# Another order for the start of a two-layer kernel: x first, weight splits inside the first stage A, no clearing of the block diagonal

## The reference

```python
# block 1: linear attention
Q, K, V = x @ Wq.T + bq, x @ Wk.T + bk, x @ Wv.T + bv
Q, K = l2_norm(Q, rows), l2_norm(K, rows)     # over the 1024 rows
tailor = 1 / (256 + Q . (sum(K) + eps))
y = x + gamma * (value_sum + Q @ (K.T @ V)) * tailor
# block 2: all 8 experts, weights = softmax of the gate, cut below 0.1, made to sum to 1
y = sum_e weights[:, e] * (x @ expert_w[e] + expert_b[e])
# block 3: 16 heads of 16 columns; scores between the heads of one row (16 x 16)
y = softmax(q @ k.T / 8) @ v, then @ Wproj.T + bproj
# block 4: router picks the 768 of 1024 rows with the highest x . w_router;
#          these rows become gelu(x @ w_block), the others stay
```

## Time and profile before

| | us |
|---|---|
| median of 3 runs | 1647.24 (1645.47 to 1650.93) |
| profiled execution | 1648.01 |
| its span, first to last instruction | 1646.3 |
| PE busy / PE weight loads | 1253.3 / 793.0 |
| DVE, ACT, POOL busy | 956.6, 671.1, 612.8 |

### The profile page before, as it was taken

One profiled execution on the slowest core, in us unless ns is written; L12 is line 12 of the kernel. 1 busy time (PEld: TensorE's weight loads), 2 busy tenths in 40 slices (PEclk: granted clock), 3 DMA queues, 4 the chain that ended last, 5 costly groups with the idle time before them and its releaser, 6 DMA issues. The chain is left out here.

```text
span 1646.3 us, 33286 instructions
## 1 busy us (share of the span) xinstructions
PE 1253.3 (76%) x12232; PEld 793.0 (48%) x12232; DVE 956.6 (58%) x2185; ACT 671.1 (41%) x1164; POOL 612.8 (37%) x890
## 2 busy tenths in 40 slices
PE   0769987988699868988699877988699886675352
PEld 0445545645375435655375445655375444442341
DVE  2143566567464856567464865567464865574545
ACT  3022345236623446236623455236623445144523
POOL 3214346135443356135343256135343355134312
PEclk9869997899779897899869997899879997698566
DMA  4000062201802063201802073201802063207220
GB/s 133 13 13 8 20 126 30 66 7 71 118 3 65 14 137 47 65 8 71 118 3 65 14 138 45 65 8 71 118 3 52 1 135 45 53 1 138 42 53 26
DMA packets 92918, 90.78 MB, mean 55 GB/s; under 512 B 7031, under 2 KB 81721, under 8 KB 92474
## 3 DMA queue, kind: packets, MB, share of 16 engines
q1 hardware_dynamic: 90170, 79.93, 24.9%
q0 software_dynamic: 2560, 8.39, 1.5%
HBM read 46.35 MB, written 41.94 MB: 54 GB/s over the span
## 5 line engine op out<-in xcount | busy, mean ns | idle before, releaser
L1410 PE MATMUL bank<-we,at 128*128 128x512 f16 x1536 | 396.4, 422 | 100.0 <-issue 52.8
L1410 PEld LDWEIGHTS bank<-we,at 128*128 128x128 f16 x1536 | 161.5, 107 | 317.6 <-issue 129.6
L513 POOL TENSOR_TENSOR part<-part 128x512 f32<-128x512 f32 x64 | 81.2, 1268 | 355.5 <-ACTq L787 355.5
L651 ACT ACTIVATE part<-bank,wexp 128x256 f32<-128x256 f32 x256 | 104.9, 471 | 208.1 <-PE bank L1410 161.5
L1130 DVE SCALAR_TENSOR_TENSOR x<-bank,wexp,x 128x256 f32<-128x256 f32 x256 | 122.9, 480 | 62.1 <-PE bank L1410 52.1
L763 ACT ACTIVATE x<-x,nm,rs 128x256 f32<-128x256 f32 x192 | 104.4, 593 | 129.8 <-POOL nm L501 129.3
L1410 PE MATMUL bank<-bt,wqkv 128*128 128x512 f16 x576 | 138.4, 382 | 18.8 <-DVE stage L975 16.8
L975 DVE TENSOR_TENSOR stage<-bank,stage 128x512 f16<-128x512 f32 x128 | 86.6, 687 | 100.5 <-ACT stage L651 100.4
L651 ACT ACTIVATE blockdiag<-shared,const 128x2048 f16<-128x2048 f16 x64 | 122.7, 1990 | 35.6 <-POOL shared L545 34.7
L494 POOL TENSOR_SCALAR nm<-mv 128x2 f32<-128x2 f32 x128 | 29.7, 232 | 260.5 <-DVE mv L1007 256.2
L651 ACT ACTIVATE stage<-bank 128x512 f16<-128x512 f32 x128 | 75.5, 597 | 123.9 <-PE bank L1410 83.2
(11 more groups left out here) (176 smaller groups left out, 2236.1 us busy)
## 6 DMA issues: line engine op xcount, KB each, us to landing
scratch_qkv<-stage SPq DMA_DIRECT2D x48, 512.0 KB, 3.4
ct<-scratch_qkv SPq DMA_DIRECT2D x128, 128.0 KB, 5.7
x_in<-in_x_dram SPq DMA_DIRECT2D x32, 256.0 KB, 2.7
keys<-scratch_qkv SPq DMA_DIRECT2D x64, 128.0 KB, 10.8
scratch_o<-stage SPq DMA_DIRECT2D x64, 128.0 KB, 3.1
bt<-scratch_o SPq DMA_DIRECT2D x16, 512.0 KB, 3.7
out_dram<-x POOLq DMA_DIRECT2D x32, 256.0 KB, 2.6
blockdiag<-in_expert_w_dram SPq DMA_DIRECT2D x1, 2048.0 KB
```

The source lines that it names most:

```text
L513: pool.tensor_tensor(part[:, 0:2, :], part[:, 0:2, :], part[:, 2:4, :], ALU.add)\
L651: return act.activation(dst, src, ACT.Copy, scale=scale)
L1410: ins = pe.matmul(dst, lhs, rhs, start=(n == 0), stop=(n == len(terms) - 1))
```

## The change

SyncE's list now starts with the four loads of x. Six loads that stage A of batch 0 needs come next, on a semaphore of their own (`w_first`); the others follow in their old order on `w_loaded`. ScalarE and VectorE enter `turn` without waiting for the weights. In the turn that has only stage A, ScalarE makes `bvr` and the first four HI halves behind TX1 and the others behind IQ; VectorE makes the LO half of `we` before the copy of NORM, three more behind it, and the others behind `a_csum`. TensorE waits for `w_first` before srow, and for all halves before CB. GpSimd no longer clears `blockdiag`; its wait for `init_p` stands alone.

```diff
@@ sync @@
-            def load(dst, src):
-                sp.dma_start(dst, src).then_inc(w_loaded, 16)
-            load(const[:, :], consts)
...
+            def load(dst, src, loaded=w_loaded):
+                sp.dma_start(dst, src).then_inc(loaded, 16)
+            for p in range(TP):
+                load_x(0, p)
+            load(const[:, :], consts, w_first)
+            load(wqk[:, :, :], wqk_t.rearrange("(k p) n -> p k n", p=P), w_first)
+            load(brow[:, :], bqk[None, :], w_first)
+            load(gam[:, :], gamma[None, :].broadcast_to([P, 1]), w_first)
+            load(wvs[:, :, :], wv.rearrange("(k p) n -> p k n", p=P), w_first)
+            load(small[:, 1, :], bv, w_first)
+            load(small[:, 0, :], w_router)
...
-            for p in range(TP):
-                load_x(0, p)
             turn(1, None, None)
@@ gpsimd @@
-            pool.wait_ge(w_hi, N_SPLITS)
-            pool.wait_ge(w_lo, N_SPLITS)
-            pool.memset(wload, 0.0).then_inc(init_p, 1)
+            pool.wait_ge(init_p, 3)
@@ scalar @@
-            act.wait_ge(w_loaded, 16 * N_LOADS)
-            act.wait_ge(init_p, 3)
-            for w, src, scale in SPLITS:
-                copy(w[:, HI, :, :], src, scale).then_inc(w_hi, 1)
...
+            def bias_rows():
+                act.wait_ge(w_first, 16 * N_FIRST)
+                copy(bvr[:, :, :], small[:, 1, :, None].broadcast_to([P, KD, P])).then_inc(bvr_ready, 1)
+
+            def split_hi(ns):
+                act.wait_ge(w_loaded, 16 * N_LOADS)
+                act.wait_ge(init_p, 3)
+                for w, src, scale in SPLITS[ns]:
+                    copy(w[:, HI, :, :], src, scale).then_inc(w_hi, 1)
+                if ns.stop is None:
+                    copy(bproj16[0:1, :], rowin[0:1, 0:D])
+                    copy(gb16[0:1, :], rowin[0:1, D:D + E], WS)
+                    copy(rowtmp[32:33, 0:D], rowin[32:33, 0:D])
+                    copy(rowtmp[32:33, D:D + E], rowin[32:33, D:D + E], WS).then_inc(w_hi, 1)
@@ scalar, turn: behind to_at_hi(a, "TX1", 1, 1) @@
+                if b is None and c is None:
+                    bias_rows()
+                    split_hi(slice(0, 4))
@@ scalar, turn: behind a_iq(a) @@
+                if b is None and c is None:
+                    split_hi(slice(4, None))
@@ vector @@
+            def split_weights(ns):
+                dve.wait_ge(w_loaded, 16 * N_LOADS)
+                for n in ns:
+                    w, src, scale = SPLITS[n]
+                    dve.wait_ge(w_hi, n + 1)
+                    dve.scalar_tensor_tensor(out=w[:, LO, :, :], in0=src, scalar=scale, in1=w[:, HI, :, :],
+                                             op0=ALU.mult, op1=ALU.subtract).then_inc(w_lo, 1)
+                if ns.stop == N_SPLITS:
...
@@ vector, turn: ahead of a_norm(a), behind it, behind a_csum(a) @@
+                if b is None and c is None:
+                    split_weights(range(0, 1))
...
+                if b is None and c is None:
+                    split_weights(range(1, 4))
...
+                if b is None and c is None:
+                    split_weights(range(4, N_SPLITS))
@@ vector, ahead of turn(0, None, None) @@
+            dve.wait_ge(w_first, 16 * N_FIRST)
@@ tensor @@
             pe.wait_ge(init_p, 3)
-            pe.wait_ge(w_hi, N_SPLITS + 1)
-            pe.wait_ge(w_lo, N_SPLITS + 1)
@@ tensor, turn: ahead of a_srow(a), and ahead of a_cb(a) @@
+                if b is None and c is None:
+                    pe.wait_ge(w_first, 16 * N_FIRST)
...
+                if b is None and c is None:
+                    pe.wait_ge(bvr_ready, 1)
+                    pe.wait_ge(w_hi, N_SPLITS + 1)
+                    pe.wait_ge(w_lo, N_SPLITS + 1)
```

More of the change, by code:

```diff
@@ L150, in build_two_layer_postln @@
         a_bank, b_bank, m_bank = banks[0:2], banks[2:4], banks[4:8]
+        w_first = sem("w_first")
         w_loaded = sem("w_loaded")
+        bvr_ready = sem("bvr_ready")
         w_hi = sem("w_hi")
@@ L339, in build_two_layer_postln, with load_x @@
         N_SPLITS = len(SPLITS)
-        N_LOADS = 16 + T
+        N_FIRST, N_LOADS = 6, 10 + T
         @block.sync
         def _(sp):
-            def load(dst, src):
-                sp.dma_start(dst, src).then_inc(w_loaded, 16)
-            load(const[:, :], consts)
-            load(wqk[:, :, :], wqk_t.rearrange("(k p) n -> p k n", p=P))
-            load(wvs[:, :, :], wv.rearrange("(k p) n -> p k n", p=P))
+            def load(dst, src, loaded=w_loaded):
+                sp.dma_start(dst, src).then_inc(loaded, 16)
+            def load_x(a, p):
+                if later(a):
+                    sp.wait_ge(xs_lo, 4 * (a - 1) + p + 1)
+                    sp.sem_inc(waits_held, 1)
+                    sp.wait_ge(a_full, a_filled(a - 1, f"TX{p}"))
+                    sp.sem_inc(waits_held, 1)
+                sp.dma_start(x_in[:, 2 * p:2 * p + 2, :], x_d[a][:, 2 * p:2 * p + 2, :])\
+                    .then_inc(x_ready[p], 16)
+            for p in range(TP):
[6 more added lines that the diff above has]
+            load(small[:, 1, :], bv, w_first)
             load(small[:, 0, :], w_router)
-            load(small[:, 1, :], bv)
-            load(brow[:, :], bqk[None, :])
-            load(gam[:, :], gamma[None, :].broadcast_to([P, 1]))
             for r in (0, 32):
@@ L364, in _ @@
                 load(ebd_in[t * E:(t + 1) * E, t, :], expert_b)
[L366 to L373, removed]
             def b_f(b, k):
@@ L975, in split_lo @@
                 return dve.tensor_tensor(dst, src, hi, ALU.subtract)
[L978 to L987, removed]
+            def split_weights(ns):
[6 more added lines that the diff above has]
+                if ns.stop == N_SPLITS:
+                    dve.wait_ge(w_hi, N_SPLITS + 1)
+                    split_lo(bproj16[32:33, :], rowin[32:33, 0:D], rowtmp[32:33, 0:D])
+                    dve.scalar_tensor_tensor(out=gb16[32:33, :], in0=rowin[32:33, D:D + E], scalar=WS,
+                                             in1=rowtmp[32:33, D:D + E], op0=ALU.mult, op1=ALU.subtract)\
+                        .then_inc(w_lo, 1)
             done_a = StepCount(A_STEPS)
```

## The result

The changed kernel takes 1609.38 us (median of 4 runs, 1606.87 to 1616.0) beside 1647.36 us for the kernel before (4 runs, 1645.47 to 1650.93). The ratio is 0.9772 (95% interval 0.9745 to 0.9798), which is 38.0 us less. The forecast was 1609.5, in a range of 1604 to 1618. A second measurement, of 6 runs, gave 1609.56 (1607.39 to 1611.67; ratio 0.978, 0.9758 to 0.9803).

A forecast was written before the change was run, and what follows sets the result against it. The prediction took a serial prologue that idles TensorE until 50.44 us as the bound. Its terms, 40.0 - 0 - 2.3 = 37.7 us off the profiled 1648.01, gave 1610.3, set to 1609.5 for the median; range 1604 to 1618.

The forecast's parts named there:

- T0: Start of TensorE's first gram matmul, forecast to move from 50.47 to 10.4 us: 40.0 us gained (39.7 to 40.6).
- Operands and weights: Stage A's operands in by 11 us, all weights by 19 to 20, before they are asked for: no cost.
- The first part: Splits of we, wqkv, wproj and wblk before the first diagonal: cost 0, bounds 0 to +1.5 us.
- thin cover: VectorE free from the first splits only 0.15 us before G; any longer chain is paid in full.
- The second part: VectorE's splits of gw, wrt, ebd and bias rows behind scaled gt delay reading M: cost 2.3 us, bounds +1 to +3.5.
- rival 1: TensorE's clock falls elsewhere in the first stage A: 1619 us if earlier, 1606.5 if no fall; 15%.
- The large form: Clock falls before the stretch of T0, T1 and TROW, which takes up to twice its 9.4 us: 1619 us.
- The rest: Everything behind the first stage A moves 37.7 us earlier, with spans between batches as before.
- Rivals 2, 3 and 4: Gaps not covering splits, 1614 to 1619, 10%; waits leaving only the clearing's gain, 1633, 3%; slower loop, up to 1715, 2%.
- Late x: Part of rival 2, in front of the first gram: GpSimd's first x late by up to 2 us; whole rival 10%.
- rival 3: A wait makes first-batch work stand for the weights; only the clearing goes, 13.8 us, 1633 us; 3%.
- The slower loop: Loop bodies run at another phase with less clock granted; at 0.76 six passes lose 106 us, 1715 us; 2%.

The follow-up runs named there:

- e5: Changed kernel with VectorE's low half of the expert weights made twice, 4.42 us more in front of NORM's copy; 1614.12 us.
- e7: Kernel with late splits and x's low halves shared between GpSimd and VectorE, with low halves of wqkv, wproj and wblk also moved behind M; 1614.41 us.
- e3: Changed kernel with VectorE's second part of the low halves made behind M, later in the first stage A; 1609.13 us.
- e2: Changed kernel with the four loads of x issued behind all the others, as before the change; 1623.3 us.
- e1: Kernel before the change with only GpSimd's clearing of the block diagonal left out; 1633.46 us, ratio 0.9923.
- g4: Late-splits kernel with a row of its own for the bias rows, plus a 2.2 us GpSimd pause before x's low halves; 1614.41 us.
- g1: Late-splits kernel with x's low halves shared and an own bias row, plus a GpSimd pause behind those halves (2.9 us meant); 1616.19 us.

## Why the prediction was right

- *T0, 40.0 us forecast, 40.6 measured.* The term came out at its lower bound (5.2 + 4.74 = 9.9): the table load ran at 0.85 us and did not wait for x, so GpSimd's memsets bind. The value taken, 5.65 for the first high half, was 1.5 us too late (3.56 + 0.63 = 4.2). The sum by the Trainium skill's figure (ScalarE: Activation LUTs, What ACT_TABLE_LOAD costs), 1.4 us worse, did not come about. That says nothing against a drain of 1.38 us: the load was over at 2.13 us and the first activation followed 1.43 us later, when x had landed, so the trace has room for one and can't show it.
- *Operands and weights of no cost.* No wait for `w_first` or `w_loaded` shows: ScalarE went from `bvr` to `we` without a gap at 30.15.
- *The first part, 0 forecast with a thin cover; 0.6 measured, inside the bound of 0 to 1.5.* VectorE was predicted free at 41.1, and the diagonal follows the last split at 41.15. But G, which bound it before, was done at 40.53, 0.6 us sooner than the splits. It stands 30.7 us behind T0, as it did before (81.22 and T0 50.47), and T0 came 0.6 us sooner than forecast, while the splits did not. So the cover was not thin but gone. e5 shows it: what is added there is paid. GpSimd's power took 2.49 us instead of 1.04, which the prediction did not have, and ended at 40.93, 0.2 us before it would have cost something. e7 shows that the splits beside it are the cause. The row that ended G before:

```profile
80.00 1.22 PE L1410 MATMUL bank<-xs,brow 1*128 1x256 f32 x2
```

- *The second part, 2.3 us.* Between `gt` and M the shift fell from 40.1 to 37.7, and e3 gets 2.1 us back inside the first stage A. M was forecast at 52.05 and read at 52.02; that the two agree to 0.03 us is luck, as T0 came 0.6 us sooner than forecast, and the way from T0 to the copy of TX1 took 0.9 us longer (19.51 instead of 18.61).
- *The clock, rival 1.* The gram matmuls took 5.28 us instead of the 4.43 of the earlier trace rows, so that 0.85 of T0's 40.6 were lost at once: the copy of TX1 is 39.7 us earlier. That they kept a slow pace longer is my reading of their durations; the column of the granted clock says 1.00 for this stretch in both traces, so it does not show it. The fall to 1.2 GHz did move: it came between 70.8 and 71.0 us before, 20.4 behind T0, and between 32.4 and 32.6 in the changed kernel, 22.7 behind T0 (windows of half a us on either side read 1.00 and 0.50). By G the 0.85 us were made up again. The large form (T0 to TROW slow) did not come: the granted clock is 1.00 from T0 to the copy of TX1. The Trainium skill (TensorE: Matmul & The Clock Gate, What's actually happening) says that the gate's timing is free-running and does not start with the kernel; the different values at the same T0, 4.61 to 5.28, agree with it.
- *The rest moves as one.* End minus w16t was 1523.9 us before and 1523.2 after. But this hides two things that cancel: seven spacings of w16t sum to 1226.1 before and 1221.4 after, and what follows them took 297.8 and 301.8. The prediction said that batch spacings would stay as they were; they stay within 1.5%. So the gain at M (37.7), at w16t (38.2) and at the end (38.9, medians 38.0) is one number only to about a us.
- *Rivals 2, 3 and 4.* Late x: e2 shows that it would cost 14 us if all of it were late. Only the clearing gone: e1, 1633.5, by chance the very figure of rival 3, but by another sum. The slower loop did not come in the changed kernel; on a small scale, 0.9 us per pass, it did in the kernels with shared x, and not by the clock alone.

**What stays open.** Which executions get the longer stretches of the lower clock behind the first stage A, and most of why the loop passes of the kernels with shared x were 0.9 us longer. The theory that the moment of the start decides on the clock was tested in two pairs, and in both the pause missed the meant moment (by 0.8 us in g4 and 2.6 in g1), so it is neither shown nor refuted. Each kernel but the changed one has one profiled execution, so chance was not separated from it either; the changed kernel's two agree (112.4 and 112.2).

## What to carry to other kernels

A start in which every engine waits for the one before it is worth unrolling: load first what the first chain needs, and let preparations run where the profile shows an engine idle; the sum can be worked out from the old trace, here to about a microsecond per term, by moving rows and asking at each whether its successor was waiting. Check each gap twice, once for the instruction's length and once for a neighbour that shares a resource with it. And when such a gain gets down to 2 us in 1600, measure it inside the stage, since the end of the program moves by more than that from one execution to the next. An instruction added ahead of a loop can change the passes of the loop too: look at them before crediting or blaming the start.

## What the runs showed of the hardware that was not expected

- VectorE's splits and GpSimd's elementwise work slow each other: four low halves 7.26 us instead of 4.48, a split 1.64 instead of 0.69, a power over 4 elements per partition 2.49 instead of 1.04.
- The same work in the same place varies with TensorE's pace: 24 gram matmuls from a standing start took 4.43 to 5.28 us (the granted clock reads 1.00 there in all of them), and the spacing of the first two batches was either 112.2 to 112.5 us (4 profiled executions) or 114.1 to 115.5 (10), with more time at 1.2 GHz in the second kind (mean granted clock of the whole spacing 0.93 to 0.94, beside 0.96 in the first kind).
- With a few instructions more at the start of the lists of VectorE and GpSimd, two fixed places of VectorE's list inside the loop idle 0.35 us longer in every pass (3.65 and 3.30, 0.58 and 0.22), alike in four kernels.
- At each of the five turns of the loop back to its start three engines stand still. TensorE idles 8.7 to 11.8 us there in the fourteen profiled executions, VectorE 8.7 to 10.9, and the profile names no releaser ("issue"). Of the changed kernel (us in total, times, longest):

```profile
PE bank L1430 <- issue: 52.0, 9, 10.5
...
DVE blockdiag L1170 <- issue: 48.9, 5, 10.0
ACT xs L651 <- issue: 48.1, 5, 9.8
```

That is some 48 us of 1607, more than the 38 that this change won. No run here takes the loop away, so what it would give back is not shown.
